# Layout of the attention products in DRAM, and the order of GpSimd's and SyncE's steps where attention meets the last stage

## What is computed

```python
# first layer: an expert MLP per batch, residual, layer norm
h = gelu(x @ Wi[e] + bi[e]);  r = h @ Wo[e] + bo[e] + x
x = layernorm(r, 1e-12) * gamma[e] + beta[e]
# second layer
x = layernorm(x) * (1 + scale) + shift          # from the time step
q, k, v = x @ Wq + bq, x @ Wk + bk, x @ Wv + bv  # 16 heads of 16
s = where(mask, -inf, q @ k.T / 4 + bias)        # bias: 8 x 16 x 512 x 512 f32
ctx = softmax(s) @ v
x = x + (ctx @ Wo + bo)
x = x + gelu2((layernorm(x) * g2 + beta2) @ W1 + b1) @ W2 + b2
```

## Time and profile before

| | |
|---|---|
| median of 3 runs | 1048.68 us (1047.84 to 1049.8) |
| the profiled execution's own time | 1049.58 us |
| its span (what the trace covers) | 1047.8 us |
| instructions | 19216 |
| PE busy | 989.4 us, 94% |
| DVE, ACT, POOL busy | 812.4, 772.8, 657.5 us |
| DMA, mean over the span | 266 GB/s, 278.63 MB |
| granted clock of PE, mean | 0.992 |

### The profile page before, as it was taken

One profiled execution on the slowest core, in us unless ns is written; L12 is line 12 of the kernel. 1 busy time (PEld: TensorE's weight loads), 2 busy tenths in 40 slices (PEclk: granted clock), 3 DMA queues, 4 the chain that ended last, 5 costly groups with the idle time before them and its releaser, 6 DMA issues.

```text
span 1047.8 us, 19216 instructions
## 1 busy us (share of the span) xinstructions
PE 989.4 (94%) x6678; PEld 738.0 (70%) x6744; DVE 812.4 (78%) x1934; ACT 772.8 (74%) x1283; POOL 657.5 (63%) x349
## 2 busy tenths in 40 slices
PE   5999999999899999999998999999998799999998
PEld 4889988898565555555555555565665599888897
DVE  5599999997878988788886888888887465655563
ACT  6755576555799999899997999999998344444444
POOL 3566766763357788778976798777876654444210
PEclk9999999999999999999999999999999899999999
DMA  8748688879989999999989999999999543221001
GB/s 228 267 153 275 230 294 282 311 261 359 349 335 421 362 391 362 381 366 351 364 326 338 342 333 376 366 356 367 318 338 254 102 109 82 81 83 41 21 22 41
DMA packets 107858, 278.63 MB, mean 266 GB/s; under 512 B 13026, under 2 KB 69090, under 8 KB 87154
## 3 DMA queue, kind: packets, MB, share of 16 engines
q1 hardware_dynamic: 107762, 277.40, 75.1%
HBM read 222.03 MB, written 55.33 MB: 265 GB/s over the span
## 4 chain that ended last, share of the span: by engine, by line
PE 55%; ACT 21%; DMA 9%; POOL 5%; DVE 5%; issue 4%; SPq 2%; DVEq 0%; ACTq 0%; POOLq 0%
PE psO L606 15%; PE psH L606 15%; ACT t_bt L937 11%; DMA t_bt<-in_fside_Bx16xSxS 8%; PE psT L722 8%; ACT t_pt L827 6%; PE psQ L606 4%; PE psS L711 4%; PE psV L735 3%; POOL t_bt L1452 3%; PE psA L606 2%; SPq L274 2%; PE psS L709 1%; ACT t_mb L959 1%; DVE t_y L1076 1%
## 5 line engine op out<-in xcount | busy, mean ns | idle before, releaser
L1452 POOL TENSOR_TENSOR t_bt<-t_bt,t_mb 128x1024 f32<-128x1024 f32 x182 | 384.5, 2145 | 115.1 <-DMA t_bt<-in_fside_Bx16xSxS 115.1
L1254 DVE CUSTOM_DVE_ANT_0 t_bt<-psS,t_bt 128x512 f32<-128x512 f32 x512 | 338.7, 686 | 85.1 <-PE psS L711 45.7
L937 ACT ACTIVATE t_bt<-t_bt,t_nm 128x512 f32<-128x512 f32 x512 | 358.4, 737 | 19.2 <-DVE t_nm L1254 18.9
L722 PE MATMUL psT<-t_idf,t_bt 128*128 128x128 f32 x2048 | 311.3, 275 | 10.5 <-ACT t_bt L937 8.9
L722 PEld LDWEIGHTS psT<-t_idf,t_bt 128*128 128x128 f32 x2048 | 251.3, 141 | 80.0 <-ACT t_bt L937 27.8
L827 ACT ACTIVATE t_pt<-psT 128x512 f32<-128x512 f32 x317 | 192.6, 608 | 16.8 <-PE psT L722 16.6
L711 PE MATMUL psS<-t_ks,t_qs 128*128 128x512 bf16 x482 | 184.2, 382 | 13.9 <-DVE t_nm L1254 9.0
L735 PE MATMUL psV<-t_pt,t_vs 128*17 128x512 f32 x1024 | 135.0, 601 | 0.0
L1264 DVE COPY t_pt<-psT 128x512 f32<-128x512 f32 x195 | 133.7, 686 | 1.3 <-PE psT L722 1.3
L711 PEld LDWEIGHTS psS<-t_ks,t_qs 128*128 128x128 bf16 x512 | 50.0, 98 | 91.0 <-DVE t_nm L1254 70.8
L864 ACT ACTIVATE psH<-psH,t_bi 128x512 f32<-128x512 f32 x64 | 42.3, 662 | 69.2 <-PE psH L606 66.3
(11 more groups left out here) (174 smaller groups left out, 1933.9 us busy)
## 6 DMA issues: line engine op xcount, KB each, us to landing
t_bt<-in_fside_Bx16xSxS SPq DMA_DIRECT2D x128, 1024.0 KB, 7.8
sc_qk<-t_parts SPq DMA_DIRECT2D x64, 384.0 KB, 6.4
t_qs<-sc_qk SPq DMA_DIRECT2D x16, 1024.0 KB, 8.0
t_ks<-sc_qk SPq DMA_DIRECT2D x16, 1024.0 KB, 10.5
t_wo_f<-in_L_cond_Wo SPq DMA_DIRECT2D x8, 1024.0 KB, 6.2
sc_qk<-t_parts SPq DMA_DIRECT2D x32, 256.0 KB, 8.4
sc_c<-t_cv SPq DMA_DIRECT2D x32, 256.0 KB
t_wi_f<-in_L_cond_Wi SPq DMA_DIRECT2D x7, 1024.0 KB, 8.7
```

Of the source, the lines that this page charges most:

```text
L722: ins = e.transpose(psT[turned_bank(n)][:, kk, :], bt[u % NB][:, t, kk * 128:(kk + 1) * 128], idf[:, :])
L937: e.activation(p, p, ACT.Exp, bias=nm[:, n % NR:n % NR + 1], scale=-1.0).then_inc(a_exp, 1)
L1254: e.tensor_tensor_reduce(bt[u % NB][:, t, :], s, bt[u % NB][:, t, :], -1.0, 3.0e38, ALU.add, ALU.min, nm[:, n % NR:n % NR + 1]).then_inc(v ...
L1452: e.tensor_tensor(bt[u % NB][:, hs, :], bt[u % NB][:, hs, :], mb[b % 2][:, hs, :], ALU.add).then_inc(g_M, 1)
```

## The change

`sc_c` becomes [batch, half, feature 16, head 8, position]: the products of a group are stored by four DMAs of 16 partitions each, without the padding and with the place in the head ahead of the head. `sc_r` gets the same form: `store_rec` stores the reciprocals 16 times, by two DMAs of 64 partitions whose source is repeated over the features. A batch is then loaded by one DMA of products and one of reciprocals, each of all 128 partitions, 512 KB. The rows of Wo are permuted in the same way before the launch. In SP's order `load_ctx(0)` is at tile 486, and `load_x2(0)`, `load_ctx(1)`, `load_x2(1)` at tile N - 14 = 498; `load_x2(2)` comes before `load_ctx(3)`. In POOL's order each batch is finished (`divide`, `low_c`, `add_bo2`) before the next begins. The waits count the new numbers of DMAs.

```diff
-        sc_c = dram("sc_c", [B, NK, 2, 4, 32, S], F32)
+        sc_c = dram("sc_c", [B, NK, HD, H // NK, S], F32)
-        sc_d, sc_r = (dram(n, [B, H, S], F32) for n in ("sc_d", "sc_r"))
+        sc_d, sc_r = dram("sc_d", [B, H, S], F32), dram("sc_r", [B, NK, HD, H // NK, S], F32)
...
-                if EARLY_C <= n < EARLY_C + 17:
-                    if n == EARLY_C:
-                        P.wait_ge(p_sc, N - 32)
-                        P.wait_ge(p_pv, UNITS // 4 - 4)
-                        P.wait_ge(g_M, masks(16 * (B - 1) - 2, 1))
-                    for i in range(2 * (n - EARLY_C), 2 * (n - EARLY_C) + 2):
-                        b, k = divmod(i, 17)
-                        if k < 16:
-                            load_ctx_part(b, k // 2, k % 2)
-                        else:
-                            load_x2(b)
+                if n == EARLY_C:
+                    P.wait_ge(p_sc, N - 32)
+                    P.wait_ge(p_pv, UNITS // 4 - 4)
+                    P.wait_ge(g_M, masks(16 * (B - 1) - 2, 1))
+                    load_ctx(0)
+                if n == N - 14:
+                    load_x2(0)
+                    load_ctx(1)
+                    load_x2(1)
...
-                load(d_cs[gi % 2], sc_c[b, hg // 2, hg % 2].rearrange("g r s -> (g r) s"), cv[gi % 2][:, :])
+                for g in range(4):
+                    load(d_cs[gi % 2], sc_c[b, hg // 2, :, 4 * (hg % 2) + g, :], cv[gi % 2][32 * g:32 * g + HD, :])
             def load_den(b):
                 for p in range(2):
-                    P.wait_ge(d_cs[p], 32 * 2 * (b + 1))
+                    P.wait_ge(d_cs[p], 80 * 2 * (b + 1))
...
             def store_rec(b):
                 P.wait_ge(v_rc, b + 1)
-                load(d_rs, sc_r[b].rearrange("h (c q) -> (h c) q", c=8), rr[:, :])
-            def load_ctx_part(b, h, rec):
-                hs = slice(HD * h, HD * h + HD)
-                if rec:
-                    P.wait_ge(d_rs, 16 * (b + 1))
-                    load(d_l[b % 2], crr[b % 2][hs, :, :], sc_r[b].rearrange("(k h) s -> h k s", k=NK)[h].unsqueeze(0).broadcast_to([HD, NK, S]))
-                else:
-                    load(d_l[b % 2], ccs[b % 2][hs, :, :], sc_c[b, :, h // 4, h % 4, 0:HD, :].rearrange("k d s -> d k s"))
+                for k in range(NK):
+                    load(d_rs, sc_r[b, k].rearrange("d h (c q) -> (h c) d q", c=8), rr[64 * k:64 * k + 64, :].unsqueeze(1).broadcast_to([64, HD, H * S // 128]))
             def load_ctx(b):
                 P.wait_ge(g_cTl, b - 1)
-                for i in range(16):
-                    load_ctx_part(b, i // 2, i % 2)
+                load(d_l[b % 2], ccs[b % 2][:, :, :], sc_c[b].rearrange("k d h s -> (d h) k s"))
+                P.wait_ge(d_rs, 32 * (b + 1))
+                load(d_l[b % 2], crr[b % 2][:, :, :], sc_r[b].rearrange("k d h s -> (d h) k s"))
...
             load_ctx(2)
-            load_ctx(3)
             P.wait_ge(v_x3, 1)
             load_x2(2)
+            load_ctx(3)
...
             divide(0)
+            low_c(0)
+            add_bo2(0)
             divide(1)
-            add_bo2(0)
-            low_c(0)
+            low_c(1)
             add_bo2(1)
-            low_c(1)
             root(crs, cmv, 1e-5, (v_var3, 1), g_rs3)
```

More of the change, by code:

```diff
@@ L950, in context_out @@
                 P.wait_ge(p_pv, gi + 1)
-                P.wait_ge(d_cs[gi % 2], 32 * (gi // 2))
+                P.wait_ge(d_cs[gi % 2], 80 * (gi // 2))
                 copy(cv[gi % 2][:, :], psV[:, :], a_cv)
@@ L1267, in reciprocals @@
                 P.wait_ge(d_dn, 16 * (b + 1))
-                P.wait_ge(d_rs, 16 * b)
+                P.wait_ge(d_rs, 32 * b)
                 e.reciprocal(rr[:, :], dn[:, :]).then_inc(v_rc, 1)
@@ L1486, in divide @@
             def divide(b):
-                P.wait_ge(d_l[b % 2], 256 * (b // 2 + 1))
+                P.wait_ge(d_l[b % 2], 32 * (b // 2 + 1))
                 e.tensor_tensor(ccs[b % 2][:, :, :], ccs[b % 2][:, :, :], crr[b % 2][:, :, :], ALU.mult).then_inc(g_cm, 1)
@@ L1588 @@
             a = np.ascontiguousarray(np.swapaxes(a.reshape(a.shape[:-1] + (NK, H // NK, HD)), -1, -2).reshape(a.shape))
+        if name == "L1_cond_Wo":
+            a = np.ascontiguousarray(np.swapaxes(a.reshape(NK, H // NK, HD, D), 1, 2).reshape(a.shape))
         if name in _COLS:
```

## The result

| | before | changed |
|---|---|---|
| median (range) | 1048.26 us (1047.73 to 1049.8), 4 runs | 1035.31 us (1033.53 to 1036.71), 4 runs |
| the profiled execution's own time | 1049.58 us | 1035.89 us |
| its span | 1047.8 us | 1034.0 us |

The ratio is 0.9881, 95% interval 0.9857 to 0.9905: 12.5 us faster, where the forecast had 9.4. The median of 1035.31 us lies 0.7 us under the low end of the forecast range, 1036.

The account below looks back on a forecast made before the run. TensorE (PE), busy 94% of the span, was taken as the bound. Gains of 2.9 + 4.9 + 2.6 = 10.4 us at the end of attention, less 1.0 us for stores, gave 9.4 us: 1039.3 us, range 1036 to 1046.5.

Parts of the forecast that it names:

- The end of attention: Last tiles to first projection: faster loads, POOL's new order and PE's kept clock together gain 10.4 us.
- the tiles from 480 to 511: Last attention tiles: bias loads land sooner, so attention ends 2.9 us earlier, with 5.0 as upper bound.
- the wait behind the last copy: Before PE's first projection: the wait of 4.9 us after the last copy out of `psT` goes.
- the first projection: PE's 24 projection matmuls: without idle time before them PE stays at 2.4 GHz, saving 2.6 us.
- The margin of 0.4 us for the root: POOL after the first projection: the root of batch 0 finds POOL just free, late by nothing, with 0.4 us to spare.
- I add 1.0 us for all seven stores in attention: Attention: the enlarged stores of the reciprocals, mostly covered by slack, cost 1.0 us in all.
- less padding when the queue is full: Attention: padding no longer written could gain at most 2 us; a bound, not in the forecast sum.
- X: SP's queue in attention: each batch's new reciprocal stores cost 2.5 us, of 0 to 3.8, against 2.4 us of slack.
- rival C: Bias loads behind reciprocal stores: stores cost over 3.8 us each, seven times; kernel slower, 1063 us if 6; chance 0.09.
- A: End of attention: PE's idle time only cut or its clock still lowered; gain 3.9 us, 1044.8 us; chance 0.14.
- B: End of attention: transfers not the reason, only the order acts and stores eat it; 1047 to 1050 us; chance 0.04.
- D: End of attention: DVE, not ACT, sets it (5.0 instead of 2.9), stores free; gain 12.5 us, 1036.2 us; chance 0.05.

Follow-up runs that it names:

- e2: Kernel before with only POOL's new order, old loads and layout: 1040.85 us, ratio 0.994.
- e1: Changed kernel with POOL's old order put back: 1036.6 us, ratio 0.9893.
- e3: Changed kernel with x2 of both batches and the products of batch 1 loaded early, at tile 486: 1038.58 us, ratio 0.9921.
- e10: Changed kernel with the reciprocals stored once and loaded by 16 small DMAs of 8 partitions a batch: 1036.13 us, ratio 0.9897.
- a_again: Changed kernel run again without any edit, against the kernel before: 1034.36 us, ratio 0.9889.
- e9: Changed kernel with the root of batch 0 put ahead of `add_bo2(1)` on POOL: 1039.39 us, ratio 0.9934.
- e4: Kernel before with the padding rows of the products not stored: 1045.84 us, ratio 0.9991.
- e12: Kernel before with the five constants' loads spread out and the padding not stored: 1041.7 us, ratio 0.9943.
- e6: Kernel before with the five constants' loads issued one at a time, tiles 266 to 330, instead of together at tile 262: 1041.16 us, ratio 0.994.
- e7: Changed kernel with the five constants' loads issued one at a time, tiles 266 to 330: 1033.12 us, ratio 0.9861.
- e13: Changed kernel with the constants' loads spread out and the reciprocals stored once, loaded by 16 small DMAs a batch: 1031.72 us, ratio 0.9856.
- e8: Changed kernel with both stores of the reciprocals doubled, the extra pair to an array nobody reads: 1044.07 us, ratio 0.9979.
- b_again: Kernel before run again without any edit, for a second profile: 1045.89 us, ratio 0.9995.

## Why the prediction was wrong, and what in it was right

**The end of attention: right.** The forecast was 10.4 us. Between tile 480 and the first `psH` the runs show 9.5 in the first pair of profiles, and 10.2 against the mean of the five old profiles. The mechanism is the one named: bias units 126 and 127 land in 7.4 and 7.9 us (forecast 6 to 8), where no small load stands in the queue. e2 and e1 part the order from the loads, and e3 shows that the place of the loads counts. That the form sets the rate is seen in the windows: 378 and 427 GB/s with large loads in e3, 208 and 198 with small ones in the kernel before and in e10. What the form alone is worth in time is not shown: no run puts all the old small loads at the new place, and e10, which puts 16 a batch there, loses only 0.3 us. In the first pair the terms are near what was forecast: the tiles from 480 to 511 are 3.1 us shorter (forecast 2.9), the wait behind the last copy falls by 4.7, from 4.9 to 0.2 (forecast 4.9), and the first projection by 2.4, from 5.4 to 3.0 (forecast 2.6). One term was put at nothing: the stretch from there to the first `psH`, taken as a fixed chain, became 0.7 us longer. The margin of 0.4 us for the root was not there, since `high_c(0)`, tied to tile 509, ended 5.2 us before the last copy, where the forecast had 6.9. Against the mean of five the terms are 4.4, 4.5, 2.1 and again 0.7 of loss; the forecast had read one execution, and not the mean.

**Attention: the step that failed.** The prediction took attention ahead of tile 480 to change by its stores alone, "I add 1.0 us for all seven stores in attention", and put what the change does at the stall near tile 275 at nothing, not having looked there. The runs show attention 2.3 us shorter instead of 1.0 longer, and nearly all of it at that stall.

The gain first. Attention up to tile 480 takes 520.3, 518.0 and 516.2 us (e2) with the old code, mean 518.2; with the new layout, in six profiles (changed, a_again, e1, e3, e9, e10), 514.9 to 516.7, mean 515.9. The scatter of the old code is as large as the difference, and e2 lies among the new ones. Of these 2.3 us, 2.1 lie in tiles 240 to 304 (71.4 against 69.3), at the stall of the constants' loads. The prediction read only the places that the change touches, and gave "less padding when the queue is full" at most 2 us of gain as a bound. The stall is such a place with a full queue. That the padding is the reason there is argued, not shown: e4 has 68.5 in these tiles and speaks for it; e12 against e6 (64.3 and 64.6) shows nothing once the stall is gone; and the timed runs of e4 and e12 don't show a gain. With the stall gone (e6 and e7) the changed layout costs attention 2 us or more, so there the charge had the right sign.

The stores of the reciprocals alone cost nothing that can be measured in the changed kernel (e10, e13), which leaves 1.0 us possible; in the kernel before they cost 4.6. My X of 2.5 us was above the mean of 1.3 to 1.6, and below the 3.1 to 5.0 of the first place. That a larger X costs much more is shown by e8: at twice the price the gain shrinks from 11.6 to 2.2 us, so rival C rested on a real mechanism. I had charged each microsecond above the slack to the end seven times over; by that rule e8 should have lost about 18 us, and it lost 9.4. So the slack is larger at some of the seven places, or the delay is partly caught up.

10.2 and 2.3 give 12.5 us; the two measured ratios give 12.5 and 11.6. The forecast lacks the 2.3, and has the 1.0 that it charged.

**The profiled execution.** 3.8 us less in attention is what the first pair of profiles shows, but 1.5 of them are the scatter of the kernel before, as its repeats tell. All executions have the stall near tile 275, but tiles 240 to 304 take 73.1 us in the one that I read, 71.2 and 69.8 in b_again and e2. For the same reason the first `psH` starts at 823.1 where I had 827: the forecast moved the rest of the trace along unchanged.

**The rivals.** A (half the gain) and B (no effect) fall with 12.5 us. C falls: X is 1.3 to 1.6 us in the mean, under its threshold of 3.9, and passes that only at the first place of e7. D (more gain: stores cost nothing, 12.5 us, 1036.2) came nearest to the time, at a chance of 0.05, but in good part by luck: the tiles end 3.1 to 4.4 us earlier, not its 5.0, its other terms, 4.9 and 2.6, gave less, and the missing 2.3 come from a place that it does not name.

**The range** ended at 1036.0, drawn at D. The bound of 2 us of gain in attention, which stood in the prediction, had not been added on top of D; with it the range would have reached to about 1034.

## What to carry to other kernels

Look at every stretch of the trace where the queue is full and the bottleneck engine idles, also where the change does nothing: its price depends on what else is in the queue. Five small loads issued together there cost the kernel before half as much as this whole change brought (6.3 against 12.5 us), and without them the change itself was worth 3 to 4 us less. Price a store with many short runs by how much later the load behind it lands, and compare that with the slack of that load. Before moving a step in a hand-written order, see what runs on the other engines at its new place.

## What the runs showed of the hardware, unexpected

**Stores with many short runs.** SP took 0.33 us to issue the store of 128 runs; for two stores with 2048 in all it took 2.47 to 6.50 in attention (changed kernel, 787.07 and 388.61) and 1.74 in the last stage (905.6); for four with 4096 it took 6.68 to 11.73 in attention. So the runs count, and the state of the queue counts as well. In the 16 us around the first such store the engines moved 349 and 282 GB/s where they moved 419 with the store of 128 runs. The Trainium skill, "DMA: Bandwidth & Descriptors", Specifications, gives 512 bytes as the least transfer for full rate and names a read-modify-write below it. The runs here are of 256 bytes and the lower rate agrees in direction; no run here tells short runs from many.

**Constants.** Four loads that read one row of 1 KB for all 128 partitions, issued together, hold up the megabyte loads behind them more than their 128 KB each explain. The window that begins some 6 us behind their issue in the kernel before shows a full share and little data; in e6 the same stretch moves 409 GB/s.

```profile
560.00:565.00 5.00, 5.00 (x40) 3.43 (x39) 4.64 (x13) 4.41 (x9) 0.00 (x0) 1.00 0.97 139
```

**DVE beside POOL.** A DVE step with two tensor operands in SBUF took 3.78 us for four instructions while POOL added two tiles, and 1.67 without; in the changed kernel a like step, with 0.9 us of overlap, took 2.38. POOL's own 2.37 us did not change. The Trainium skill, "SBUF — State Buffer", section "SBUF: two separate sides", describes a port pair that such an operation and a GpSimd operation hold in turn. The durations agree roughly: 2.1 us more at an overlap of 2.3, and 0.7 more at 0.9.

**The clock.** e7 has the same waits of PE around the first `psX` as the changed kernel (1.3, 1.1 and 0.9 us), yet the granted clock falls in one and not in the other, and 24 `psH` take 7.23 us instead of 5.83. In e7:

```profile
820.00:825.00 5.00, 4.30 (x13) 3.45 (x14) 2.72 (x6) 1.65 (x3) 5.00 (x3) 0.66 0.21 53
```

e3 has the same waits too, and its 24 `psH` take 7.37 us; in the six other profiles with these waits, the changed kernel's two among them, they take 5.8. The clock also falls in e1, e6, e9 and e12. What decides it, with gaps this short, stays open.
